# A Mamba block and a mixture of experts on one core: Silu of u and z made back to back, z projected ahead of dt, B and C, and the first softplus piece of a block three slots later

## What is computed

```python
# layer 1, Mamba: d_inner 512, 16 states per channel, conv of 4 taps, rank 16
u, z  = split(xn @ W_in.T)
u_c   = silu(causal_conv(u, conv_w) + conv_b)
dt, B, C = split(u_c @ W_xp.T)
dt    = softplus(dt @ W_dt.T + b_dt)
h_t   = exp(dt_t * A) * h_(t-1) + dt_t * u_t * B_t      # per channel and state
y     = (h . C) + u_c * D
x     = x + (y * silu(z)) @ W_out.T
# layer 2, mixture of experts: 8 experts, the best 2 per token
gate, up, down of the token's two experts, silu(gate) * up, weighted by softmax of the two logits
```

## Time and profile before

| | |
|---|---|
| median of 3 runs | 2322.84 us (2321.6 to 2324.49) |
| profiled execution, own time | 2327.84 us |
| its span | 2325.9 us |
| busy in the span | PE 77%, weight loads 40%, DVE 81%, ACT 78%, POOL 83% |
| DMA | 159 GB/s in the mean, queues busy for 58% (SP) and 7.5% (POOL) |
| mean granted TensorE clock | 0.888 of full speed |

### The profile page before, as it was taken

One profiled execution on the slowest core, in us unless ns is written; L12 is line 12 of the kernel. 1 busy time (PEld: TensorE's weight loads), 2 busy tenths in 40 slices (PEclk: granted clock), 3 DMA queues, 4 the chain that ended last, 5 costly groups with the idle time before them and its releaser, 6 DMA issues.

```text
span 2325.9 us, 32531 instructions
## 1 busy us (share of the span) xinstructions
PE 1795.3 (77%) x7694; PEld 923.0 (40%) x7694; DVE 1893.7 (81%) x2437; ACT 1806.5 (78%) x3753; POOL 1933.7 (83%) x1190
## 2 busy tenths in 40 slices
PE   5566768697878788797878788797878788666785
PEld 2112323153534344353434444353434344343542
DVE  0389988899889888899889888899889888999221
ACT  5888888888898788888998788888998787763332
POOL 1588897989999898999999898999999898987333
PEclk9888978797989898998989898997989898786998
DMA  1635454477777786677777786677777786797332
GB/s 57 145 83 141 105 141 109 125 177 184 169 178 178 169 213 160 170 183 184 174 175 180 163 218 157 171 183 180 176 179 178 160 221 147 183 259 221 70 49 34
DMA packets 217979, 369.34 MB, mean 159 GB/s; under 512 B 31040, under 2 KB 86592, under 8 KB 217664
## 3 DMA queue, kind: packets, MB, share of 16 engines
q1 hardware_dynamic: 192208, 333.56, 58.1%
q0 software_dynamic: 25584, 33.71, 7.5%
HBM read 285.05 MB, written 83.01 MB: 158 GB/s over the span
## 4 chain that ended last, share of the span: by engine, by line
issue 23%; POOL 23%; ACT 18%; PE 18%; DVE 9%; DMA 8%; POOLq 0%; ACTq 0%; DVEq 0%; SPq 0%
DMA out<-yt,xt 8%; POOL arena L1324 8%; DVE dA L1116 5%; PE ring L603 5%; ACT dA L979 4%; POOL arena L1332 4%; POOL out L1372 3%; POOL sorted_x L1362 2%; PE yps L697 2%; PE ring L611 2%; DVE arena L1116 2%; POOL arena L1347 2%; POOL arena L1342 1%; PE p_g L729 1%; PE ring L640 1%
## 5 line engine op out<-in xcount | busy, mean ns | idle before, releaser
L1324 POOL TENSOR_TENSOR arena<-arena,b_bc 128x2048 f32<-128x2048 f32 x256 | 998.4, 3900 | 88.3 <-PE yps L697 88.3
L979 ACT ACTIVATE dA<-arena,a_s 128x512 f32<-128x512 f32 x1024 | 680.5, 684 | 116.0 <-DVE arena L1125 69.9
L1116 DVE TENSOR_TENSOR_SCAN dA<-dA,arena 128x512 f32<-128x512 f32 x384 | 454.5, 1213 | 156.8 <-ACT dA L979 107.3
L1116 DVE TENSOR_TENSOR_SCAN dA<-dA,carry,arena 128x512 f32<-128x512 f32 x384 | 477.6, 1274 | 52.3 <-POOL arena L1324 36.2
L697 PE MATMUL yps<-arena,const_s 128*32 128x512 f32 x2048 | 320.4, 702 | 59.9 <-POOL arena L1332 35.9
L1332 POOL TENSOR_TENSOR arena<-arena,c_bc 128x511 f32<-128x511 f32 (+1 forms) x256 | 335.0, 1308 | 28.3 <-DVE arena L1116 26.5
L1125 DVE TENSOR_TENSOR arena<-dA,c_bc 128x1024 f32<-128x1024 f32 x256 | 313.6, 1225 | 8.8
L1372 POOL DMA_INDIRECT out<-yt,xt x135 | 215.0, 1592 | 115.7 <-ACT yt L1020 84.1
L595 PE MATMUL ring<-arena 128*128 128x512 f32 x488 | 265.4, 670 | 55.5 <-ACT arena L883 21.6
L729 PEld LDWEIGHTS p_g<-xT,w_e 128*128 128x128 f32 x1680 | 216.7, 209 | 127.5 <-issue 127.5
L603 PE MATMUL ring<-arena 128*128 128x512 f32 x480 | 236.8, 639 | 35.3 <-ACT arena L883 13.6
(11 more groups left out here) (171 smaller groups left out, 2973.5 us busy)
## 6 DMA issues: line engine op xcount, KB each, us to landing
arena<-dt_d SPq DMA_DIRECT2D x512, 256.0 KB
w_e<-in_w_moe SPq DMA_DIRECT2D x105, 512.0 KB, 4.7
dt_d<-arena SPq DMA_DIRECT2D x128, 256.0 KB, 2.4
w_e<-in_w_moe SPq DMA_DIRECT2D x105, 256.0 KB
xt<-sorted_x SPq DMA_DIRECT2D x135, 129.0 KB
b_bc<-bc_d SPq DMA_DIRECT2D x256, 64.0 KB, 2.4
c_bc<-bc_d SPq DMA_DIRECT2D x256, 64.0 KB, 5.3
xs<-in_x SPq DMA_DIRECT2D x16, 512.0 KB, 4.4
```

Source lines behind the costliest of these rows:

```text
L979: act.activation(dA[:, j, :], rep_dt[:, c % 2, j, :], ACT.Exp, scale=a_s[:, n, j:j + 1]).then_inc(s_exp, 1)
L1116: return dve.tensor_tensor_scan(out_ap, dA[:, j, :], hs[:, u % 3, j, :], init, ALU.mult, ALU.add)
L1324: pool.tensor_tensor(hs[:, u % 3], rep_dtu[:, c % 2], b_bc[:, g, :].unsqueeze(1).to_broadcast([P, J, T]), ALU.mult).then_inc(s_dbu, 1)
```

## The change

Block 1 and later: z is projected and taken in slots 5 to 7 (before: 7 to 9), in the order Z0, Z2, Z1, Z3. P0 is made in slot 8 and taken in slot 9 (before: slots 5 and 6), and D0 is made in slot 9 and taken with E0 in slot 10 (before: 6 and 7). SU goes from slot 5 and SZ from slot 10 to slot 8, one directly behind the other. L0 goes from slot 8 to 11, and E1 from slot 11 to 12. On POOL the first piece's four steps go from slots 7, 8, 9 and 10 to 10, 11, 12 and 12. On SP the store of the first piece goes from slot 12 to 13, that of B and C from 7 to 10, and the two parts of the first copy-back from 12 and 13 to 13 and 14.

```diff
-MAKES = {... (-12, 4): ["W3"], (-11, 2): ["P0"], (-10, 3): ["D0"], (-9, 1): ["Z0"], (-8, 1): ["Z2"],
-         (-8, 3): ["Z1"], (-7, 0): ["Z3"], (-6, 0): ["D1"], ...
+MAKES = {... (-12, 4): ["W3"], (-11, 2): ["Z0"], (-10, 0): ["Z2"],
+         (-10, 2): ["Z1"], (-9, 0): ["Z3"], (-8, 4): ["P0"], (-7, 3): ["D0"], (-6, 0): ["D1"], ...

-TAKES = {... (-11, 1): ["W3"], (-11, 2): ["SU"], (-10, 1): ["P0"], (-9, 0): ["D0", "E0"], (-9, 3): ["Z0"],
-         (-8, 0): ["L0"], (-8, 1): ["Z2"], (-7, 0): ["Z1"], (-7, 4): ["Z3"], (-6, 0): ["SZ"], (-6, 1): ["D1"],
-         (-5, 1): ["E1"], (-3, 0): ["L1"], ...
+TAKES = {... (-11, 1): ["W3"], (-11, 4): ["Z0"], (-10, 1): ["Z2"],
+         (-10, 4): ["Z1"], (-9, 1): ["Z3"], (-8, 1): ["SU", "SZ"], (-7, 1): ["P0"], (-6, 0): ["D0", "E0"],
+         (-6, 1): ["D1"], (-5, 0): ["L0"], (-4, 1): ["E1"], (-3, 0): ["L1"], ...
@@ sync
-                for p, k in pieces(s, (-4, -1, 1, 6), (-10, -1, 3, 6)):
+                for p, k in pieces(s, (-3, -1, 1, 6), (-10, -1, 3, 6)):
                     store_dt(p, k)
-                if q >= 0 and front and n == 7 or s == -13:
+                if q >= 0 and front and n == 10 or s == -13:
                     store_bc(q + 1)
-                if q >= 0 and front and n == 12 or s == -9:
+                if q >= 0 and front and n == 13 or s == -9:
                     load_rep(q + 1, 0, (0, 1))
-                if q >= 0 and front and n - 1 == 12 or s == -9:
+                if q >= 0 and front and n - 1 == 13 or s == -9:
                     load_rep(q + 1, 0, (2, 3))
@@ gpsimd
-                for p, k in pieces(s, (-8, -3, 0, 2), (-11, -1, 1, 2)):
+                for p, k in pieces(s, (-5, -3, 0, 2), (-11, -1, 1, 2)):
                     less_lost(p, k)
-                for p, k in pieces(s, (-7, -2, 0, 4), (-11, -1, 1, 4)):
+                for p, k in pieces(s, (-4, -2, 0, 4), (-11, -1, 1, 4)):
                     plus_relu(p, k)
-                for p, k in pieces(s, (-9, -4, -1, 1), (-12, -3, 0, 1)):
+                for p, k in pieces(s, (-6, -4, -1, 1), (-12, -3, 0, 1)):
                     round_off(p, k)
-                for p, k in pieces(s, (-6, -2, 0, 4), (-11, -1, 1, 4)):
+                for p, k in pieces(s, (-4, -2, 0, 4), (-11, -1, 1, 4)):
                     dtu(p, k)
```

## The result

The changed kernel takes 2548.15 us (median, 2544.9 to 2553.6), and the kernel before 2323.66 us beside it. The ratio is 1.096, with an interval of 1.094 to 1.099. The forecast was 2464 us: the sign was right, and the loss of 224 us was predicted as 141. The profiled execution has a span of 2542.4 us, at a mean granted clock of 0.857. One execution of one experiment took 3590.6 us where its other one took 2531.7 us; it is left out, so that this experiment rests on a single time.

The account below looks back on a forecast made before the run. Each block was taken as bounded by DVE's stretch, then POOL's. Losses of 49 + 16 + 25 + 51 = 141 us on the profiled 2327.8 gave 2468.8, forecast as 2464 us because that execution lay 5.0 above the median; range 2385 to 2500.

Parts of the forecast that it names:

- step 1: Slots 5 and 6: ACT waits for PE's Z0 ahead of quarter 2's `decay`, delaying DVE's scan; 49 us lost.
- step 2: POOL's softplus piece: `round_off` moves from slot 7, where POOL waits anyway, into its gapless stretch; 16 us lost.
- step 3: Slot 10: POOL's late scatters wait for ACT's second weight, behind D0 and E0; 25 us lost, bounds nothing and 36.
- step 4: First piece's copy-back lands late, POOL's drive waits 3.4 us a block, counted in full; 51 us, bounds 0 and 68.
- My bound of 7.0 us: Longer of two transfer times, 4.9 and 7.0 us, taken for the landing of the copy-back's second part.
- The pair at nothing: Both Silus together in slot 8 cost nothing, since ACT has room while DVE is busy with the sorting's small operations.
- grouping pays: Rival: Silu pair leaves the recurrence alone, DVE's 31.9 us of waits for quarter 3 go; 2291 us, chance 0.1.
- Copies in time: Rival: the first three losses hold but the copy-back's landing is hidden; 2413 us, chance 0.25.
- More of the slow clock: Rival: PE's idling in slots 8 and 9 brings the lower clock to slot 5 of all 15 blocks; 2500 us, 0.12.
- The model of two stretches: Block time is DVE's stretch, slots 3 to 8, some 44 us, plus POOL's, slot 8 to next slot 3, some 84.

Follow-up runs that it names:

- the late take: Changed kernel with ACT taking Z0 at place 0 of slot 6, behind quarter 2's exponential, and Z1 at the start of slot 7: 2486.3 us.
- the second weight first: Changed kernel with ACT writing the second weight of slot 10 ahead of D0 and E0 instead of behind them: 2513.3 us.

## Why the prediction was wrong

The sum again, each term with what the runs give for it:

| term | forecast | measured | from |
|---|---|---|---|
| step 1, Z0 | 49 | 48 to 51 | stretch 1 with and without the late take |
| held routing operations | none | 25 to 28 | stretch 1 with and without `route` moved |
| step 2, `round_off` | 16 | 16 | 1.05 us in the timeline, not undone alone; stretch 2 agrees |
| step 3, second weight | 25 | 30 | stretch 2 of its run |
| step 4, copies | 51 | 78 to 89 | the stretches of its run |
| sum | 141 | 197 to 214 | 218 in the loop |

These are means over blocks 4 to 13, and those of stretch 1 mix blocks of different clocks.

**The failed steps are step 4's landing, and a term that was missing.** In step 4 the issues were right to 0.1 us. The landing was taken from two transfers of 64 KB for a part of four transfers of 256 KB. My bound of 7.0 us was no bound: the four land 5.1 to 7.8 us behind their issues, each later than the one before it. The queue of SP keeps the DMA engines busy for 91% of the 22 us around the wait, which would hold the last copies up. But where the earlier trace rows were read they were as busy (96.6% from 1089 to 1092 us), so it isn't the load that differs. That it is the size, and what stands ahead in the queue, is argued and was not tested. In the mean the wait was 5.0 us for 3.4. The step also stopped at the drive. Behind it ACT and PE had to catch up as well, 1.3 us a block in the fourth stretch, and "the wait counts in full" was too little.

```profile
q1 hardware_dynamic: 2792, 4.87, 91.0%
arena<-dt_d SPq DMA_DIRECT2D x8, 256.0 KB, 5.4
```

These are rows of the DMA view from 1199 to 1221 us (packets, MB, share of 16 engines; KB each, median us to landing).

**The missing term.** I moved DVE's slot 6 by 2.9 us against POOL and asked only who waits for whom. What overlaps whom was not asked. The kernel before already held the warning: in 2 of its 16 blocks the same operation takes 2.2 and 3.7 us, and 0.6 and 0.9 us in two more, which is why its mean is 587 ns at a usual 170.

**Step 1 was right** in mechanism: in block 7 the scan of quarter 2 starts 5.0 us behind the start of gate and up, for 5.1 forecast. Its size came out in the mean, with some luck. The wait is 3.7 us in most odd blocks, as said, but 6.3 in most even ones, and the blocks with the slow clock are others than in the kernel before. The reading of the table loads was right: ACT lost 37.8 us for 38 forecast. **Step 2** is visible at its place (1180.55 us in block 7, with no gap around it). With the second weight first, stretch 2 is 24.26 us, and 26.46 - 3.36 + 1.05 = 24.15. **Step 3** was a little small: from block 3 on the scatter waits 1.7 us in odd and 2.6 to 3.2 us in most even blocks, 2.4 in the mean of all 14, for 0.8 and 2.4 in turn.

**The pair at nothing** was too kind. The cover, DVE's small operations in slot 8, is thinner than I took it for: with `route` in slot 7, 1.8 us more on ACT comes out at POOL's drive. The pair costs 12 us there.

**The rivals.** That grouping pays (2291 us, and with it the rule that activations of one table set belong together) fell. The Trainium skill ("ScalarE: Activation LUTs", "Table sets: the hidden batching unit") says to batch by table set and counts the loads that this saves. The trace agrees: 30 instructions fewer on ACT. It just wasn't time of this kernel. Copies in time fell in the other direction. More of the slow clock isn't needed for the sum, and isn't there in slot 5: in blocks 3 to 14 its gate and up matmuls are over 2.3 us long in 5 of 12 blocks after and in 6 before. In slot 11 it is 12 for 10. No run tested what the clock costs by itself.

**The model of two stretches** served for what the change added, but not for what might be taken away. A stretch that looks gapless on one engine can have the next one 1 to 2 us behind it.

## What to carry to other kernels

When a change shifts one engine against another, list which operations will newly overlap, not only which will wait. An operation that is held shows as a long instruction, not as idle time, and a mean far above the usual length of the group is its trace. Saving work on an engine off the path brought nothing here. Bunching it delayed whoever waits behind the bunch, even though the total was less. The landing of a late transfer is best taken from rows of its own size and place in the queue, and its cost followed until every engine has caught up. A mean over blocks is to be compared at the same clock.

## What the runs showed of the hardware

DVE's small operations on SBUF were held until POOL's running tensor operation ended, every time that they met, in all 16 traces: the gap operation 169 times, for up to 3.8 us where it takes 0.17 alone, ending 0.01 to 0.03 us behind POOL's; `hot` 61 times, ending 0.08 to 0.09 us behind. The shorter product at line 1332 holds the gap operation for 0.7 us. Held were a subtraction and a comparison of two SBUF tensors, and an operation of one tensor of 8 elements with a scalar (15 of 15, and once one of 4 elements). Not held were the maximum, the index search, the same scalar operation on one element, and products and scans with one operand in PSUM, such as this product by C in the kernel before while the drive runs from 1023.78 to 1027.59:

```profile
1023.37 1.23 DVE L1125 TENSOR_TENSOR arena<-dA,c_bc 128x1024 f32<-128x1024 f32 x1
```

The Trainium skill ("SBUF — State Buffer", "Who interferes with whom") says that DVE and GpSimd share a pair of ports, that an operation with two SBUF inputs or in a 2-port mode (which `tensor_scalar` can enter) contends for it, and that whoever comes first blocks the other for its whole instruction. All that was held here fits it, and the ends of the operations agree to 0.1 us. That the 8-element operation ran in such a mode is what the Trainium skill allows and no run shows, and neither does any show POOL held by DVE. I had not looked for it, as the kernel before hardly shows it.
